# A fused transformer block on one core: loads of the opening split over two queues, and products of zeros while the weights load

## The chip, the core and the metric

The kernel runs on one core of a Trainium2 chip. The metric is the device time of one execution in microseconds, and lower is better. Before the change it is 466.33 us (median of 3 runs, 465.85 to 466.46).

## What is computed

x is 16 x 64 x 512 (1,024 tokens of width 512), the context is 16 x 512 x 512, all float32. Three residual stages follow each other, each on a layer norm of x:

```python
x = x + cross_attention(layernorm(x), ctx, top_k=32)
x = x + wave_attention(layernorm(x))
x = x + ternary_ffn(layernorm(x))
```

Only the first one matters for the change:

```python
q = query @ Wq.T + bq
k = mem_state @ Wk.T + bk
v = mem_state @ Wv.T + bv
scores = einsum('btd,bsd->bts', q, k) * scale
vals, idx = top_k(scores, 32)
scores = masked.at[b_ix, t_ix, idx].set(vals)
attn = softmax(scores)
return einsum('bts,bsd->btd', attn, v) @ Wo.T + bo
```

The wave attention convolves deposits over time with a kernel made of three small parameter vectors (frequency, damping, phase) and mixes its 16 heads by a 16 x 16 coupling matrix.

## The kernel before

The kernel is written out engine by engine. Every engine has its own program, in a fixed order, and the programs meet at semaphores. A wait on an engine holds back all that stands behind it on that engine.

Queries and keys are never formed apart. TensorE first multiplies the two weight matrices into one, M1 = Wq.T Wk (512 x 512), in four steps over slices of 128 rows: `m1_step(o)` (line 1265) waits until query slice o and key slice o (256 KB each) have landed, and issues four float32 products of 128 x 512 into banks 0 to 3. M1 is then split into a high part (ScalarE, `m_hi`, line 521) and a low part (VectorE, `m_lo`, line 843), and `q_product(n)` (lines 1250 to 1252) multiplies it with the transposed, normalised tokens. `q_product(0)` waits for each of the four low parts in turn.

TensorE's order in the opening is: m1_step 0, 1, 2; `turn_first` 0 to 3 (line 1257: transposes of the normalised token tiles `xn`); m1_step 3; two tiny groups (lines 1287, 1288) for a bias; turn_first 4 and 5; q_product(0); turn_first 6 and 7; q_product(1) and so on.

Tokens come in eight tiles of 128, loaded two at a time (`resid<-x`, 512 KB). For each, VectorE makes the statistics (lines 826, 828, 830), GpSimd the factor (lines 391, 393), ScalarE the normalised tile `xn` (line 503), TensorE turns it, ScalarE takes the high part (`xt_hi`, line 509) and VectorE the low part (`xt_lo`, line 835).

VectorE's order in the opening is:

```python
dve.wait_ge(par_in, 64)
dve.tensor_reduce(nmax[0:H, :], cpl[0:H, :], AX.X, ALU.max, negate=True).then_inc(cmax_ok, 1)
absolute(d, wpar[:, 1, :]).then_inc(sp_u, 1)
for o in range(DC):
    sumk_part(o)
    first_stats((2 * o, 2 * o + 1))
first_xt((0, 1, 2, 3))
for e in range(DC):
    m1_lo_part(e)
```

`par_in` counts the four small tables of the wave attention: `wpar` (three vectors, 8 KB each as spread over the partitions) and `cpl` (1 KB). `sumk_part(o)` (lines 859, 860) adds up key slice o, scaled by the bias columns in `cols` (6 KB), and waits for query and key slice o. GpSimd waits for `par_in` too, and then makes `targ` (lines 384, 386).

ScalarE's order: an activation table load (before line 514), two small exponentials (514, 516), xn 0 to 5, xt_hi 0 to 3, xn 6 and 7, four m_hi, xt_hi 4 to 7, then the parts of qT (line 538) between absolute sums of the feed-forward weights (`wab`, line 551).

All transfers are requested by SyncE, in program order: `first_loads(o)` for o = 0 to 3 (lines 280 to 287), three chunks of w1 (line 293, 1 MB each), `woraw` and a bias (303, 304), then the context (line 311).

Of the kernel before, what the change touches and what calls it, by code (L numbers as in the profile page):

```python
# [13 lines left out]
P = 128  # L14
# [3 lines left out]
H = 16  # L18
# [5 lines left out]
DC = D // P  # L24
# [15 lines left out]
def perceiver_kernel(nc, x, ctx, wq, wk, wv, woT, bo, wgT, bg, freq, damp, phase, coup, woutT, bout, w1T, w2T, b2,  # L40
                     small, out):
    st = ExitStack()
    with st:
# [27 lines left out]
        def f(ap):  # L71

            return ap.bitcast(F32)
# [11 lines left out]
        mix_hi = sb("mix_hi", [P, P], F32R)  # L85
# [15 lines left out]
        cols = sb("cols", [P, 3, DC])  # L101
# [56 lines left out]
        bank = [st.enter_context(nc.psum_tensor(f"bank{n}", [P, 512], F32)) for n in range(8)]  # L158

        small_in, tab_in, bo_in, wo_in, wv_in = map(sem, ("small_in", "tab_in", "bo_in", "wo_in", "wv_in"))
        wst_in = [sem(f"wst_in{n}") for n in range(4)]
        wab_in = [sem(f"wab_in{n}") for n in range(3)]
        wqk_in = [sem(f"wqk_in{n}") for n in range(DC)]
# [5 lines left out]
        consts, par_in, tpos_ok = sem("consts"), sem("par_in"), sem("tpos_ok")  # L170
# [39 lines left out]
        def rows(w):  # L210
            return w.rearrange("(c p) n -> p c n", p=P)
# [63 lines left out]
        @block.sync  # L275
        def _(sp):

            def first_loads(o):

                sp.dma_start(wqraw[:, o, :], rows(wq)[:, o, :]).then_inc(wqk_in[o], 16)  # L280
                sp.dma_start(wkraw[:, o, :], rows(wk)[:, o, :]).then_inc(wqk_in[o], 16)
                if o == 0:
                    sp.dma_start(cols[:, :, :], small[0]).then_inc(small_in, 16)
                    for n, a in enumerate((freq, damp, phase)):
                        sp.dma_start(wpar[:, n, :], a.partition_broadcast(P)).then_inc(par_in, 16)
                    sp.dma_start(cpl[0:H, :], coup).then_inc(par_in, 16)
                sp.dma_start(resid[:, 2 * o:2 * o + 2, :], x_v[:, 2 * o:2 * o + 2, :]).then_inc(x_in[o], 16)

            def abs_load(k):

                if k >= 3:
                    sp.wait_ge(abs_ok, k - 2)
                sp.dma_start(w_place(k, wab[:, k % 3, :]), w_chunk(k)).then_inc(wab_in[k % 3], 16)

            def ternary_load(k):

                sp.dma_start(w_place(k, wst[:, k % 4, :]), w_chunk(k)).then_inc(wst_in[k % 4], 16)

            for o in range(DC):
                first_loads(o)  # L300
            for k in range(3):
                abs_load(k)
            sp.dma_start(woraw[:, :, :], rows(woT)).then_inc(wo_in, 16)
            sp.dma_start(bias_x[:, :], bo.partition_broadcast(P)).then_inc(bo_in, 16)

            for b in range(B):
                for c in range(SC):
                    if b >= 4:
                        sp.wait_ge(ctx_turned, DC * (b - 3))
                        sp.wait_ge(nat_lo_ok, SC * (b - 4) + c + 1)  # L310
                    sp.dma_start(ctxr[:, b % 4, c, :], rows(ctx[b])[:, c, :]).then_inc(ctx_in[b % 4], 16)
                if b == 1:
                    for k in range(3, 2 * DC):
                        abs_load(k)
                    sp.dma_start(wvraw[:, :, :], rows(wv)).then_inc(wv_in, 16)
                if b == 3:
                    sp.dma_start(b1c[:, :], small[1]).then_inc(tab_in, 16)
                    sp.dma_start(bqg[:, :, :], small[2]).then_inc(tab_in, 16)

            for s, n in enumerate((2, 3, 0, 1)):  # L320
                sp.wait_ge(ctx_turned, DC * (B - 3 + s))
                sp.wait_ge(nat_lo_ok, SC * (B - 3 + s))
                sp.dma_start(wgraw[:, s, :, :], rows(wgT[n])).then_inc(wg_in[n], 16)
            sp.wait_ge(mt_used, 2 * DC * NT)
            sp.dma_start(bkb[:, :], bg[0].partition_broadcast(P)).then_inc(kvb_in, 16)
            sp.dma_start(bvb[:, :], bg[1].partition_broadcast(P)).then_inc(kvb_in, 16)
            for k in range(2 * DC):
                if k < 4:
                    sp.wait_ge(wg_lo_ok[w_slot(k)], DC)
                else:  # L330
                    sp.wait_ge(tern_ok, k - 3)
                ternary_load(k)
            sp.wait_ge(v_ps, NT)
            sp.dma_start(woutraw[:, :, :], rows(woutT)).then_inc(wout_in, 16)
            sp.dma_start(bias_o[:, :], bout.partition_broadcast(P)).then_inc(bout_in, 16)
            sp.wait_ge(conv_ps, H)
            sp.dma_start(bias_2[:, :], b2.partition_broadcast(P)).then_inc(b2_in, 16)
            for t in range(NT):
                sp.wait_ge(final_ok, t + 1)
                sp.dma_start(out_v[:, t, :], resid[:, t, :]).then_inc(stored, 16)  # L340
            sp.wait_ge(stored, 16 * NT)
# [3 lines left out]
        def _(pool):  # L345
            steps = [0]

            def link(ins):

                steps[0] += 1  # L350
                ins.then_inc(pool_step, 1)
                pool.wait_ge(pool_step, steps[0])

            link(pool.memset(ident[:, :], 0.0))
            pool.affine_select(out=ident[:, :], in_=ident[:, :], compare_op=ALU.not_equal, fill=1.0, base=0,
                               pattern=[[-1, P]], channel_multiplier=1).then_inc(consts, 1)
            pool.memset(neg_half[:, :], -0.5).then_inc(consts, 1)
            pool.memset(half_pi[:, :], TWO_PI / 4).then_inc(consts, 1)
            pool.memset(ones[:, :], 1.0).then_inc(consts, 1)  # L360
            pool.wait_ge(consts, 4)
            pool.tensor_tensor(fold[:, :], ident[:, 0:T], ident[:, T:P], ALU.add).then_inc(consts, 1)

            pool.wait_ge(consts, 5)
            for q in range(2):
                if q:
                    pool.wait_ge(tpos_ok, q)
# [128 lines left out]

        @block.scalar
        def _(act):
            def ln_apply(n, t, to):  # L500

                act.wait_ge(ln_rstd, 2 * n + 2)
                act.activation(to, resid[:, t, :], ACT.Identity, bias=ln_nb[:, n:n + 1],  # L503
                               scale=ln_rs[:, n:n + 1]).then_inc(ln_ready, 1)
# [60 lines left out]
            q_part(4)  # L565
            q_part(5)
            act.wait_ge(arg_ok, 1)
            act.wait_ge(consts, 5)
            act.activation(targ[:, :, :], targ[:, :, :], ACT.Sin, bias=half_pi[:, :], scale=-1.0).then_inc(cos_ok, 1)
            abs_part(4)  # L570
            q_part(6)
# [236 lines left out]
        def _(dve):  # L808
# [30 lines left out]
            d, u, z, z2, q, a = (wtmp[:, n, :] for n in range(6))  # L839
# [65 lines left out]
            for part in (PI_HI, PI_MID, PI_LO):  # L905
# [6 lines left out]
            link(dve.tensor_scalar(cpl[0:H, :], cpl[0:H, :], rinv[0:H, 0:1], None, ALU.mult))  # L912
            dve.tensor_copy(cpr[0:H, :].rearrange("p (h e) -> p h e", e=E8),
                            cpl[0:H, :].unsqueeze(2).to_broadcast([H, H, E8])).then_inc(cpr_ok, 1)
            dve.wait_ge(consts, 5)
            dve.tensor_reduce(mask8[:, :], ident[:, :].rearrange("p (h e) -> p e h", e=E8), AX.X,
                              ALU.add).then_inc(cpr_ok, 1)

# [328 lines left out]
        def _(pe):  # L1247
# [22 lines left out]
            def turn_first(t):  # L1270
# [3 lines left out]
                    pe.wait_ge(xt_lo_ok, t - 1)  # L1274
                turn(turn_bank(t), first_xn(t)).then_inc(xn_turned, 1)

            for o in range(DC - 1):
                m1_step(o)
            pe.wait_ge(consts, 5)
            for t in range(4):  # L1280
                turn_first(t)
            m1_step(DC - 1)
# [3 lines left out]
            for e in range(DC):  # L1286
                pe.matmul(bank[4][:, e:e + 1], sum_k[:, token(e)], ones[:, :], start=True, stop=True)
            pe.matmul(bank[4][:, DC:DC + 1], bqk1[:, :].to_broadcast([P, P]), ones[:, :], start=True,
                      stop=True).then_inc(qbias_ps, 1)
            def q_product(n):  # L1290
# [6 lines left out]
                for e in range(DC):  # L1297
                    if n == 0:
# [15 lines left out]
                      stop=True).then_inc(u_ps, 1)  # L1314
# [439 lines left out]
```

## Time and profile before

| | before |
|---|---|
| median of 3 runs | 466.33 us (465.85 to 466.46) |
| the profiled execution | 466.23 us |
| its span, first to last instruction | 464.5 us |
| TensorE busy | 447.9 us, 96% |
| VectorE, ScalarE, GpSimd busy | 70%, 55%, 49% |
| chain that ended last | TensorE 67%, VectorE 19%, ScalarE 5% |

The span is shorter than the execution's own time by what lies around the first and the last instruction, 1.7 us. The shares are averages over stages with different limits; how the first 24 us go is read from the timeline.

### The profile page before, as it was taken

Reading aid. Unit: us, or ns where it says so; the run is one execution under the profiler, and the core shown is the slowest. Engines: PE = TensorE matmul, PEld = TensorE weight load, DVE = VectorE, ACT = ScalarE, POOL = GpSimd, SP = SyncE. Lnnn points to the kernel's source line nnn. Section 1 sums busy time; section 2 is a strip of 40 time slices with the busy share of each in tenths; the row PEclk is TensorE's granted clock in tenths of the full one; section 3 lists DMA queues with packets and bytes.
Section 4 is the critical chain, followed back from the end, with each engine's and each line's share of the span. In section 5 each row is a group of like instructions: output and inputs, shape, how many; then the busy total and the mean of one; then the engine's idle time right before and its main releaser. Section 6 shows DMA issues by size and latency. Waiting matters only on the chain.

```text
span 464.5 us, 6292 instructions
## 1 busy us (share of the span) xinstructions
PE 447.9 (96%) x2146; PEld 352.8 (76%) x2146; DVE 326.9 (70%) x594; ACT 253.3 (55%) x392; POOL 226.2 (49%) x265
## 2 busy tenths in 40 slices
PE   6999989899999999889999999999999999999996
PEld 2588655588888888678888888888788888888884
DVE  4899679699999999978998893655872223522224
ACT  1777949577878887765787446443541221111111
POOL 6703098497779777834001761334226643333330
PEclk9999999999999999999999999999999999999999
DMA  7997733253444342570880300000000000100002
GB/s 222 414 370 286 260 105 113 69 159 122 127 138 131 118 117 90 182 226 1 338 289 11 110 1 23 1 0 0 2 0 0 1 0 1 68 23 1 0 1 91
DMA packets 23327, 48.94 MB, mean 105 GB/s; under 512 B 2688, under 2 KB 2688, under 8 KB 22272
## 3 DMA queue, kind: packets, MB, share of 16 engines
q1 hardware_dynamic: 23296, 48.55, 30.8%
q8 instruction: 17, 0.28, 0.2%
q14 instruction: 14, 0.11, 0.1%
HBM read 46.44 MB, written 2.10 MB: 105 GB/s over the span
## 4 chain that ended last, share of the span: by engine, by line
PE 67%; DVE 19%; ACT 5%; issue 4%; POOL 2%; DMA 2%; DVEq 0%; SPq 0%; ACTq 0%
PE bank L1250 10%; PE bank L1252 10%; PE bank L1251 10%; PE bank L1697 6%; PE bank L1699 6%; PE bank L1683 6%; PE bank L1684 6%; DVE mt_lo L1005 4%; PE bank L1265 4%; DVE work L1018 3%; DVE mx L1014 3%; PE bank L1257 2%; POOL nat_lo L428 2%; PE bank L1343 2%; DVE s_t L1025 1%
## 5 line engine op out<-in xcount | busy, mean ns | idle before, releaser
L428 POOL TENSOR_TENSOR nat_lo<-ctxr,nat_hi 128x512 fp32r<-128x512 f32 x64 | 83.9, 1338 | 21.0 <-ACT nat_hi L612 20.6
L801 ACT ACTIVATE g<-bank,b1c 128x512 f32<-128x512 f32 x32 | 22.1, 689 | 92.2 <-PE bank L1699 92.2
L1230 DVE CAST g_hi<-g 128x512 fp32r<-128x512 f32 x32 | 13.9, 434 | 74.9 <-ACT g L801 74.8
L483 POOL TENSOR_SCALAR w2s<-w2t 128x512 fp32r<-128x512 int8 x32 | 19.9, 621 | 65.9 <-PE bank L1684 65.9
L1697 PE MATMUL bank<-xt_lo,w1s 128*128 128x512 f32 x128 | 50.8, 397 | 0.0
L1699 PE MATMUL bank<-xt_hi,w1s 128*128 128x512 f32 x128 | 50.7, 396 | 0.0
L1683 PE MATMUL bank<-w2s,g_lo 128*128 128x512 f32 x128 | 50.2, 392 | 0.2 <-DVE g_lo L1232 0.2
L1684 PE MATMUL bank<-w2s,g_hi 128*128 128x512 f32 x128 | 50.2, 392 | 0.0
L588 ACT ACTIVATE mt_hi<-bank 128x512 fp32r<-128x512 f32 x64 | 37.8, 595 | 18.6 <-PE bank L1423 18.2
L1005 DVE TENSOR_TENSOR mt_lo<-bank,mt_hi 128x512 fp32r<-128x512 f32 x64 | 43.5, 681 | 4.7 <-ACT mt_hi L588 4.4
L1423 PEld LDWEIGHTS bank<-ident,ctxr 128*128 128x128 f32 x256 | 30.5, 141 | 12.9 <-issue 4.9
L612 ACT ACTIVATE nat_hi<-ctxr 128x512 fp32r<-128x512 f32 x64 | 36.6, 624 | 5.6 <-PE bank L1455 5.6
L1423 PE MATMUL bank<-ident,ctxr 128*128 128x128 f32 x256 | 38.6, 275 | 0.6 <-DMA ctxr<-ctx 0.4
L1437 PE MATMUL bank<-mt_lo,qs 128*128 128x512 f32 x64 | 30.3, 473 | 0.0
L391 POOL TENSOR_TENSOR ln_rs<-ln_ve,neg_half 128x1 f32<-128x1 f32 x24 | 14.6, 606 | 32.2 <-DVE ln_ve L830 31.7
L503 ACT ACTIVATE xn<-resid,ln_nb,ln_rs 128x512 f32<-128x512 f32 x24 | 19.3, 814 | 19.1 <-POOL ln_nb L393 18.6
L1683 PEld LDWEIGHTS bank<-w2s,g_lo 128*128 128x128 f32 x128 | 24.0, 188 | 6.0 <-issue 0.6
L1699 PEld LDWEIGHTS bank<-xt_hi,w1s 128*128 128x128 f32 x128 | 24.0, 188 | 5.6
L1684 PEld LDWEIGHTS bank<-w2s,g_hi 128*128 128x128 f32 x128 | 24.0, 188 | 5.6
L1697 PEld LDWEIGHTS bank<-xt_lo,w1s 128*128 128x128 f32 x128 | 24.0, 188 | 5.5
L1453 PE MATMUL bank<-nat_lo,at 128*128 128x512 f32 x64 | 25.3, 395 | 1.4 <-issue 0.9
L472 POOL TENSOR_TENSOR qfT<-qfT,gate 128x512 f32<-128x512 f32 x8 | 10.4, 1296 | 32.7 <-ACT gate L769 32.7
(234 smaller groups left out, 1205.8 us busy)
## 6 DMA issues: line engine op xcount, KB each, us to landing
ctxr<-ctx SPq DMA_DIRECT2D x64, 256.0 KB, 2.8
wab<-w1T SPq DMA_DIRECT2D x4, 1024.0 KB, 10.4
wab<-w2T SPq DMA_DIRECT2D x4, 1024.0 KB, 5.7
wgraw<-wgT SPq DMA_DIRECT2D x4, 1024.0 KB, 5.3
wst<-w1T SPq DMA_DIRECT2D x4, 1024.0 KB, 7.6
wst<-w2T SPq DMA_DIRECT2D x4, 1024.0 KB, 7.1
resid<-x SPq DMA_DIRECT2D x4, 512.0 KB, 6.3
out<-resid SPq DMA_DIRECT2D x8, 256.0 KB, 2.2
```

The source lines that it names most:

```text
L428: pool.tensor_tensor(nat_lo[:, par, c, :], ctxr[:, b % 4, c, :], f(nat_hi[:, par, c, :]), ALU.subtract).then_inc(nat_lo_ok, 1)
L588: act.activation(mt_hi[:, g % 4, :], ctx_bank(g)[:, :], ACT.Copy).then_inc(mt_hi_ok, 1)
L612: act.activation(nat_hi[:, par, c, :], ctxr[:, b % 4, c, :], ACT.Copy).then_inc(nat_hi_ok, 1)
L1005: dve.tensor_tensor(mt_lo[:, g % 4, :], ctx_bank(g)[:, :], f(mt_hi[:, g % 4, :]), ALU.subtract).then_inc(mt_lo_ok, 1)
L1250: pe.matmul(to, w_hi, x_lo, start=first, stop=False)
L1251: pe.matmul(to, w_lo, x_hi, start=False, stop=False)
L1252: return pe.matmul(to, w_hi, x_hi, start=False, stop=last)
L1423: ins = pe.transpose(ctx_bank(g)[:, token(c)], ctxr[:, b % 4, c, token(d)], ident[:, :])
L1683: pe.matmul(to, g_lo[:, n % 2, token(k)], w2s[:, n % 2, :], start=(c == 0), stop=False)
L1684: ins = pe.matmul(to, g_hi[:, n % 2, token(k)], w2s[:, n % 2, :], start=False, stop=(c == FC - 1))
L1697: pe.matmul(bank[n % 2][:, :], w1s[:, n % 2, d, :], xt_lo[:, d, half(n // FC)], start=(d == 0), stop=False)
L1699: ins = pe.matmul(bank[n % 2][:, :], w1s[:, n % 2, d, :], xt_hi[:, d, half(n // FC)], start=False, stop=(d == DC - 1))
```

## The change

ScalarE requests the four key slices and the five small tables, ahead of everything else in its program: key slice 0, the tables, key slices 1 to 3. SyncE requests the query slices and x in the order q0, x0, q1, q2, x1, q3, x2, x3. GpSimd first sets the tile `mix_hi` (128 x 128) to zero, and TensorE multiplies that tile by itself five times, in float32, into bank 7, before it waits for the first slices. The semaphore `consts` therefore counts one step more. `mix_hi` gets its real content much later (line 948), and bank 7 is written afresh by turn_first(3).

```diff
-            def first_loads(o):
+            def query_load(o):
 
                 sp.dma_start(wqraw[:, o, :], rows(wq)[:, o, :]).then_inc(wqk_in[o], 16)
-                sp.dma_start(wkraw[:, o, :], rows(wk)[:, o, :]).then_inc(wqk_in[o], 16)
-                if o == 0:
-                    sp.dma_start(cols[:, :, :], small[0]).then_inc(small_in, 16)
-                    for n, a in enumerate((freq, damp, phase)):
-                        sp.dma_start(wpar[:, n, :], a.partition_broadcast(P)).then_inc(par_in, 16)
-                    sp.dma_start(cpl[0:H, :], coup).then_inc(par_in, 16)
+
+            def x_load(o):
+
                 sp.dma_start(resid[:, 2 * o:2 * o + 2, :], x_v[:, 2 * o:2 * o + 2, :]).then_inc(x_in[o], 16)
...
-            for o in range(DC):
-                first_loads(o)
+            query_load(0)
+            x_load(0)
+            query_load(1)
+            query_load(2)
+            x_load(1)
+            query_load(3)
+            x_load(2)
+            x_load(3)
...
+            pool.memset(f(mix_hi[:, :]), 0.0).then_inc(consts, 1)
             link(pool.memset(ident[:, :], 0.0))
...
         @block.scalar
         def _(act):
+            def key_load(o):
+
+                act.dma_start(wkraw[:, o, :], rows(wk)[:, o, :]).then_inc(wqk_in[o], 16)
+
+            key_load(0)
+            act.dma_start(cols[:, :, :], small[0]).then_inc(small_in, 16)
+            for n, a in enumerate((freq, damp, phase)):
+                act.dma_start(wpar[:, n, :], a.partition_broadcast(P)).then_inc(par_in, 16)
+            act.dma_start(cpl[0:H, :], coup).then_inc(par_in, 16)
+            for o in range(1, DC):
+                key_load(o)
+
...
+            pe.wait_ge(consts, 1)
+            for n in range(5):
+                pe.matmul(bank[7][:, 0:P], f(mix_hi[:, :]), f(mix_hi[:, :]), start=True, stop=True)
             for o in range(DC - 1):
                 m1_step(o)
-            pe.wait_ge(consts, 5)
+            pe.wait_ge(consts, 6)
```

SyncE's requests at the start of its program, before (`wqraw`, `wkraw` are query and key slices, `resid` the tokens, `wab` the w1 chunks):

```order
L280 DMA wqraw<-wq 128x512
L281 DMA wkraw<-wk 128x512
L283 DMA cols<-attn_bias_cols 128x12
L285 DMA wpar<-freq 128x16
L285 DMA wpar<-damp 128x16
L285 DMA wpar<-phase 128x16
L286 DMA cpl<-coup 16x16
L287 DMA resid<-x 128x2x512
L280 DMA wqraw<-wq 128x512
L281 DMA wkraw<-wk 128x512
L287 DMA resid<-x 128x2x512
```

and of the changed kernel:

```order
L280 DMA wqraw<-wq 128x512
L284 DMA resid<-x 128x2x512
L280 DMA wqraw<-wq 128x512 x2
L284 DMA resid<-x 128x2x512
L280 DMA wqraw<-wq 128x512
L284 DMA resid<-x 128x2x512 x2
L290 DMA wab<-w1T 128x2048 x3
```

The nine requests of keys and tables are gone from this queue, and the first x stands second instead of eighth.

ScalarE at the start of its program in the changed kernel (before, it began with the table load):

```order
L506 DMA wkraw<-wk 128x512
L509 DMA cols<-attn_bias_cols 128x12
L511 DMA wpar<-freq 128x16
L511 DMA wpar<-damp 128x16
L511 DMA wpar<-phase 128x16
L512 DMA cpl<-coup 16x16
L506 DMA wkraw<-wk 128x512 x3
L530 ACT_TABLE_LOAD
L530 ACTIVATE wtmp<-wtmp 128x16 [waits sp_u]
```

`cpl`, the last table, is the sixth request of its queue here and was the seventh of SyncE's, and the table load now stands behind nine requests.

## Rows read from the trace of the kernel before

**Rows 1.** The page, part 1: busy time and share of the span
```profile
PE 447.9 (96%) x2146; PEld 352.8 (76%) x2146; DVE 326.9 (70%) x594; ACT 253.3 (55%) x392; POOL 226.2 (49%) x265
```
**Rows 2.** Timeline from 0 to 24: SyncE's requests (start us, us, queue line, tile)
```profile
0.79 0.37 SPq L280 DMA_DIRECT2D wqraw<-wq  x1
1.22 0.42 SPq L281 DMA_DIRECT2D wkraw<-wk  x1
...
3.58 0.43 SPq L286 DMA_DIRECT2D cpl<-coup  x1
...
5.03 0.43 SPq L281 DMA_DIRECT2D wkraw<-wk  x1
...
8.35 0.64 SPq L281 DMA_DIRECT2D wkraw<-wk  x1
```
**Rows 3.** DMA issues at 1.2, 3.6 and 5.0 us: KB, us to landing
```profile
wqraw<-wq SPq DMA_DIRECT2D x1, 256.0 KB, 2.4
wkraw<-wk SPq DMA_DIRECT2D x1, 256.0 KB, 2.9
...
cpl<-coup SPq DMA_DIRECT2D x1, 1.0 KB, 2.6
...
wkraw<-wk SPq DMA_DIRECT2D x1, 256.0 KB, 4.6
```
**Rows 4.** Windows: busy PE, PEld, DVE, ACT, POOL; PEclk, DMA share, GB/s
```profile
4.00:5.00 1.00, 0.84 (x1) 0.50 (x2) 0.32 (x2) 0.00 (x0) 0.00 (x0) 1.00 0.13 14
...
10.00:11.00 1.00, 1.00 (x4) 0.38 (x3) 0.93 (x4) 0.00 (x0) 0.92 (x2) 1.00 1.06 387
```
**Rows 5.** Timeline: TensorE's weight loads in m1_step 0 and 1
```profile
5.17 0.34 PEld L1265 LDWEIGHTS bank<-wkraw,wqraw 128*128 128x128 f32 x1 [0.52 <-issue]
6.03 0.34 PEld L1265 LDWEIGHTS bank<-wkraw,wqraw 128*128 128x128 f32 x1 [0.52 <-issue]
...
8.59 0.34 PEld L1265 LDWEIGHTS bank<-wkraw,wqraw 128*128 128x128 f32 x1 [0.52 <-issue]
9.28 0.19 PEld L1265 LDWEIGHTS bank<-wkraw,wqraw 128*128 128x128 f32 x1 [0.36 <-issue]
9.71 0.19 PEld L1265 LDWEIGHTS bank<-wkraw,wqraw 128*128 128x128 f32 x1 [0.24 <-DMA wkraw<-wk]
```
**Rows 6.** Timeline: VectorE from the tables on, GpSimd beside it
```profile
6.32 0.16 DVE L873 TENSOR_REDUCE nmax<-cpl 16x1 f32<-16x16 f32 x1 [1.67 <-DMA cpl<-coup]
6.36 2.18 POOL L384 TENSOR_TENSOR targ<-wpar,tpos 128x1152 f32<-128x1152 f32 x1 [3.11 <-DMA cpl<-coup]
...
6.49 2.34 DVE L859 TENSOR_SCALAR sum_k<-wkraw,cols 128x512 f32<-128x512 f32 x1
...
26.36 0.47 DVE L859 TENSOR_SCALAR sum_q<-wqraw,cols 128x512 f32<-128x512 f32 x1
```
**Rows 7.** Timeline: the way to m_hi (ScalarE) and m_lo (VectorE)
```profile
18.02 0.82 ACT L503 ACTIVATE xn<-resid,ln_nb,ln_rs 128x512 f32<-128x512 f32 x1 [0.62 <-POOL ln_nb L393]
...
22.06 2.07 ACT L521 ACTIVATE m_hi<-bank 128x512 fp32r<-128x512 f32 x4
...
22.70 2.48 DVE L843 TENSOR_TENSOR m_lo<-bank,m_hi 128x512 fp32r<-128x512 f32 x4 [0.86 <-ACT m_hi L521]
```
**Rows 8.** The chain that ended last, from 22 to 44 us (start, us, what)
```profile
22.35 0.79 PE bank L1287 x8
...
24.29 0.24 PE bank L1250
...
43.55 1.28 ACT L569
```
**Rows 9.** Timeline: GpSimd's first memset, ScalarE's table load and first activation
```profile
0.79 0.20 POOL L355 MEMSET ident<- 128x128 f32 x1 [0.29 <-POOLq L1744]
0.80 1.28 ACT L514 ACT_TABLE_LOAD   x1 [0.80 <-PEq L1744]
...
6.59 0.21 ACT L514 ACTIVATE wtmp<-wtmp 128x16 f32<-128x16 f32 x1 [4.52 <-DVE wtmp L822]
```

More of the change, by code:

```diff
@@ L360, in _ @@
             pool.memset(ones[:, :], 1.0).then_inc(consts, 1)
-            pool.wait_ge(consts, 4)
+            pool.wait_ge(consts, 5)
             pool.tensor_tensor(fold[:, :], ident[:, 0:T], ident[:, T:P], ALU.add).then_inc(consts, 1)
-            pool.wait_ge(consts, 5)
+            pool.wait_ge(consts, 6)
             for q in range(2):
@@ L567, in _ @@
             act.wait_ge(arg_ok, 1)
-            act.wait_ge(consts, 5)
+            act.wait_ge(consts, 6)
             act.activation(targ[:, :, :], targ[:, :, :], ACT.Sin, bias=half_pi[:, :], scale=-1.0).then_inc(cos_ok, 1)
@@ L914, in _ @@
                             cpl[0:H, :].unsqueeze(2).to_broadcast([H, H, E8])).then_inc(cpr_ok, 1)
-            dve.wait_ge(consts, 5)
+            dve.wait_ge(consts, 6)
             dve.tensor_reduce(mask8[:, :], ident[:, :].rearrange("p (h e) -> p e h", e=E8), AX.X,
```

## The prediction

> **What bounds the kernel now.** I read the views from the whole to the place of the change: the page's busy shares, the timeline of the first 24 us by engine, the time from request to landing of single transfers, DMA traffic by microsecond, and the chain that ended last.
>
> TensorE is busy for 96% of the span [rows 1], so only time at the front that TensorE really gets back, or waits of others that end earlier, can shorten the run. In the opening four things matter.
>
> First, SyncE requests everything: query slice 0 at 0.79, key slice 0 at 1.22, then five small tables, the last (cpl) at 3.58, and the next key slice only at 5.03 [rows 2]. Key slice 0 lands 2.9 us after its request, 4.12; cpl 2.6 after, 6.18; key slice 1 4.6 after, 9.63 [rows 3]. By 8.35 a request costs 0.64 us instead of some 0.4 [rows 2]. Between 4 and 5 us the DMA engines move 14 GB/s, while from 10 to 11 they move 387 [rows 4]. That hole is the time in which SyncE asked for tables.
>
> Fourth, there is a second path, through VectorE. It waits for the last table, starts at 6.32, spends 2.34 us on the first row sum (line 859) while GpSimd runs line 384 from 6.36 to 8.54, and goes on, hardly pausing, through the row sums and the statistics of the eight tiles [rows 6]. The same row sum alone takes 0.47 [rows 6]. ScalarE follows with xn 5 at 18.02 and, behind the high parts of xT and two more xn, reaches m_hi at 22.06. VectorE makes the first m_lo from 22.70 on [rows 7]. Four take 2.48, so the first is done at about 23.3. TensorE's q_product(0) needs it and starts at 24.29 [rows 8]. With 0.3 us for the semaphore and a weight load (0.19), it could have started at 23.6 to 23.7. So VectorE's path has **0.65 us of slack** to TensorE's, no more.
>
> After that TensorE's products lead the chain until ScalarE takes over with its table load at 43.55 [rows 8], and the chain goes through ScalarE and VectorE into the attention. Whatever q_product(0) gains is therefore handed on; I find no fixed clock or transfer behind it that would stop it.
>
> **The change part by part.** My sum is made against the profiled execution, 466.23 us with a span of 464.5; the median of the runs is 466.33, so I add 0.10 at the end. A difference of 0.2%, 0.93 us, is about what a measurement here can tell.
>
> *Key slice 0 by ScalarE.* No row shows a transfer requested by ScalarE. It is free at 0.80 (its table load starts there [rows 9]), and a request costs SyncE 0.37 to 0.64 [rows 2]. Query and key slices are then asked for at about 0.8 each. The query slice took 2.4, the key slice behind it 2.9 [rows 3], so both lie between 3.2 and 3.7. I take 3.6: 0.56 before 4.16. The ends are a gain of 0.96, and nothing if the two hinder each other.
>
> *Zeros.* GpSimd's memset of mix_hi stands first; its neighbour on ident, of the same size, takes 0.20 from 0.79 [rows 9], so TensorE starts at about 1.1. Five products are ten records. The lower bound is line 1287's record, 0.79/8 = 0.10 us at the full clock, twice that at the low one: 2.0 us in all. The upper bound is a quarter of 0.86 (128 columns for 512) plus a bare weight load of 0.34: 0.55 each, 5.5 us. In rows 5 the loads run beside the products, so I take 2.1 and an end at 3.2, before the slices. At 5.5 the real work would start at 6.6 with the clock up, and end within 0.1 us of today. If 4.95 us of work raise the clock here too, it rises at 6.05. From 3.6 that leaves 2.45 slow us, which hold 2.85 records; 21.15 at 0.43 end at 15.1, where today's 24 records end at 17.0. **TensorE's path gains about 1.9.** If the zeros do not count, it gains the 0.56 of the start alone. The multiplied values are never read: bank 7 is overwritten.
>
> *Data for that pace.* TensorE would want slice 1 at about 8.4, slice 2 at 11.8, and slice 3 after the four turns at 17. ScalarE asks for key slice 1 seventh, at 0.8 + 6 x 0.47 = 3.6. If the two queues share the 387 GB/s evenly, key 1 (256 KB at half of that, 1.35 us) lands near 7. If everything is served in order of request, 2.5 MB come before its end, 6.8 us at 387 from 2.4 on: 9.2. That would cut TensorE's gain to 1.1. Query 3 and x are requested 4 to 5 us earlier than today.
>
> *Tables by ScalarE.* cpl is the sixth request of its queue, not the seventh: 0.48 earlier. That is the upper end for VectorE's path. For the lower end, a request costing 0.64 each time would put cpl at 4.3 (0.7 later), and traffic on the other queue, which these tables did not meet before (they ran through the hole), could add what key 1 shows over key 0, 1.7. Nearest is cpl's own row, 2.6, with the same key slice ahead of it; I add 0.23 for the new neighbour. **VectorE's path gains 0.25**, with ends of +0.48 and -2.4.
>
> *What waits behind ScalarE's nine requests.* Its table load (1.28) ends at 0.8 + 9 x 0.47 + 1.28 = 6.3, and its first activation started at 6.59 [rows 9], behind VectorE. The normalisations need it only past 11. Nothing is lost there. GpSimd's 0.2 us is hidden too: it waits for the tables until 6.36. SyncE reaches the w1 loads 5 us earlier, and nobody needs those before 29.
>
> *Sum.* TensorE could be at q_product(0) at 24.29 - 1.9 = 22.4, but m_lo allows it only 0.65 + 0.25 = **0.9 us** earlier than now. Hence 466.23 - 0.9 = 465.33, plus 0.10: 465.4. Of the 1.9 us that the opening seems to offer, a full microsecond stops at VectorE's path.
>
> **The rivals.**
>
> *A. Shared DMA engines delay the tables: slower.* Both queues end on the same 16 engines. For it speaks that the tables now compete with 2.5 MB of x and queries; against it, that a table of 1 KB and a slice of 256 KB take about the same time to land, 2.6 and 2.4 to 2.9, so that a request alone is latency and hardly engine time [rows 3]. Suppose that the engines alternate whole requests. At 387 GB/s 256 KB last 0.68 and x 1.35. Between 3.8 and the fifth table stand x 0, queries 1 and 2, x 1 and query 3: 4.7 us, so cpl lands near 8.5, 2.3 later than now. Minus the slack of 0.65 this makes the kernel 1.65 slower: 468.0. A milder sharing with cpl at 7.2 costs 0.4. The point of decision is cpl's landing at 6.8. The Trainium skill, DMA: Bandwidth & Descriptors, section Queues, rings and completion order, says that an engine serves the queues in turn and drains a whole packet from one before it switches; by that rule the result would be this rival's. Chance 0.16.
>
> *B. About nothing, 466.1.* The tables land up to 0.5 later than now, or key slice 1 comes at 9.5 (TensorE's gain 0.9, less with a zeros block that ends late). A gain of 0 to 0.5. Chance 0.24.
>
> *C. VectorE's path gets shorter, 464.7.* If VectorE's first row sum comes in ahead of GpSimd's line 384, it takes 0.47 and not 2.34, and the slack becomes 2.5; TensorE's path then decides, with 1.9 at most and 1.6 with a little late data. Against it: both wait for the same tables, and VectorE has two small instructions ahead of that sum, as now. Chance 0.14.
>
> *Forecast.* A gain of 0.6 to 1.13 us, 465.2 to 465.7. Chance 0.46.
>
> **How the numbers follow.** The forecast's interval is cut by the 0.93 us in its upper part, so 0.30 of its 0.46 I count as faster; with C that makes 0.44. The rest of it and B make 0.40, and A 0.16. The range goes from C's 464.7 to the milder form of A, 466.8; outside are A's hard form and a gain above 1.6.
>
> **What would show it.** Right: ten zero records from about 1.1 to 3.2; m1_step at 3.6; 0.43 per record from about 6; VectorE's line 873 a few tenths before 6.32; **TensorE idle ahead of the first q_product, released by m_lo**, which is the mark of this prediction. Wrong: no such wait (C, or TensorE's path was slower than worked out), line 873 later than 6.8 (A), a wait for key slice 1 past 9.4, or slow records as long as before, which would mean that zeros do not raise the clock.

## The result and the profile after

The changed kernel takes **470.42 us** (median of 4 runs, 470.1 to 471.23), against 466.38 for the kernel before, measured again beside it (465.85 to 466.46). The ratio is 1.0087, with a 95% interval of 1.0069 to 1.0106: **4.0 us slower**, where 0.9 faster was forecast. The profiled execution took 470.54 us with a span of 468.7. The page of the changed kernel, part 1 (busy time and share of the span), answers to [rows 1]:

```profile
PE 451.3 (96%) x2156; PEld 354.8 (76%) x2156; DVE 325.0 (69%) x594; ACT 253.4 (54%) x392; POOL 226.4 (48%) x266
```

The shares tell nothing: TensorE's 3.4 us of additional busy time are for the most part the ten records of zeros (2.5). The loss has to be found in the opening.

DMA issues of the changed kernel, three narrow stretches from 0.8, 3.3 and 3.9 us on (KB, us from request to landing), beside [rows 3]:

```profile
wkraw<-wk ACTq DMA_DIRECT2D x1, 256.0 KB, 3.1
wqraw<-wq SPq DMA_DIRECT2D x1, 256.0 KB, 3.5
...
wqraw<-wq SPq DMA_DIRECT2D x1, 256.0 KB, 8.7
cpl<-coup ACTq DMA_DIRECT2D x1, 1.0 KB, 7.2
...
resid<-x SPq DMA_DIRECT2D x1, 512.0 KB, 10.8
wkraw<-wk ACTq DMA_DIRECT2D x1, 256.0 KB, 7.9
```

SPq marks SyncE's requests, ACTq ScalarE's. cpl holds 1 KB. It took 2.6 us before and takes 7.2 now. Key slice 1 took 4.6 and takes 7.9. The first pair lands at 3.9 (key) and 4.3 (query), so it is complete 0.2 us later than before (4.12). What the two queues ask for lands side by side: bias columns and x 0 at 5.6 and 5.8, frequency and query 1 at 7.7 and 7.5, damping and query 2 at 8.9 and 8.4, phase by itself at 9.8, cpl and x 1 at 10.5 and 10.7, key 1 and query 3 at 11.8 and 12.0.

The timeline of the changed kernel by engine (start us, us, engine, line): ScalarE's requests, TensorE's weight loads, and VectorE and GpSimd from the tables on. It answers to [rows 2, 5, 6]:

```profile
0.79 0.41 ACTq L506 DMA_DIRECT2D wkraw<-wk  x1
...
1.05 2.21 PEld L1295 LDWEIGHTS bank<-mix_hi 128*128 128x128 f32 x10 [1.05 <-POOL mix_hi L358]
...
3.32 0.52 ACTq L512 DMA_DIRECT2D cpl<-coup  x1
...
3.87 1.67 ACTq L506 DMA_DIRECT2D wkraw<-wk  x3
...
4.36 0.50 PEld L1281 LDWEIGHTS bank<-wkraw,wqraw 128*128 128x128 f32 x2 [1.10 <-DMA wqraw<-wq]
...
8.79 0.28 PEld L1281 LDWEIGHTS bank<-wkraw,wqraw 128*128 128x128 f32 x1 [0.52 <-issue]
9.32 0.19 PEld L1281 LDWEIGHTS bank<-wkraw,wqraw 128*128 128x128 f32 x1 [0.24 <-issue]
10.59 0.16 DVE L889 TENSOR_REDUCE nmax<-cpl 16x1 f32<-16x16 f32 x1 [4.59 <-DMA cpl<-coup]
10.63 2.11 POOL L388 TENSOR_TENSOR targ<-wpar,tpos 128x1152 f32<-128x1152 f32 x1 [7.23 <-DMA cpl<-coup]
10.67 2.10 DVE L838 SCALAR_TENSOR_TENSOR wtmp<-wpar 128x16 f32<-128x16 f32 x1
...
11.86 0.30 PEld L1281 LDWEIGHTS bank<-wkraw,wqraw 128*128 128x128 f32 x2 [2.35 <-DMA wkraw<-wk]
...
12.69 0.47 DVE L875 TENSOR_SCALAR sum_k<-wkraw,cols 128x512 f32<-128x512 f32 x1
```

VectorE's chain starts at 10.59, released by cpl, and not at 6.32: 4.27 us late. TensorE is late on its own account too: key slice 1 releases it at 11.86, not 9.71. And the zeros, which run from 1.05 to 3.26, did nothing for the clock: the loads still last 0.34 until 8.8 and the clock rises at about 9.0, within 0.1 us of where it rose before. (That the two are so close is a coincidence of two executions, as the experiments show.) The collision with GpSimd is there as before, only that it now hits the small instruction of line 838 (2.10) and spares the row sum (0.47), the other way round than in [rows 6]; the sum of the two is about the same (2.57 against 2.49).

The chain that ended last in the changed kernel, the pieces that matter (start, length, what), answers to [rows 8]:

```profile
3.32 7.16 DMA cpl<-coup
...
27.04 0.70 DVE m_lo L859
27.88 0.47 PE bank L1266
...
47.37 1.28 ACT L585
```

The chain runs through VectorE's path, as forecast for the gain: cpl, statistics, xn, m_hi, m_lo. TensorE waits 0.9 us for m_lo and starts q_product(0) at 27.88. By the timeline it started at 24.05 before, which is 3.83 earlier (24.29, in [rows 8], is where the chain view lets that piece begin). The line of the kernel before and that of the changed one:

```profile
24.05 0.48 PE L1250 MATMUL bank<-xt_lo,m_hi 128*128 128x512 f32 x1
```

```profile
27.88 0.47 PE L1266 MATMUL bank<-xt_lo,m_hi 128*128 128x512 f32 x1 [0.93 <-DVE m_lo L859]
```

The table load of ScalarE follows 3.82 later than before. VectorE's first top-8 is 3.78 late (69.67 and 73.45), so the delay is handed on undiminished. It is 3.6 at 176 us and 4.2 from 186 us to the end. What adds 0.6 there need not be this change: measured by the same top-8 steps against the same profile of the kernel before, the kernel with the zeros alone goes from 1.16 to 1.75 late in that stretch, while the one with eight ones, below, shows no step (0.51 early on both sides). Its cause is open.

Windows of the changed kernel (busy PE, PEld, DVE, ACT, POOL; granted clock, DMA share, GB/s) answer to [rows 4]:

```profile
6.00:7.00 1.00, 1.00 (x2) 0.34 (x1) 0.00 (x0) 0.85 (x1) 0.00 (x0) 1.00 0.39 110
...
8.00:9.00 1.00, 1.00 (x3) 0.48 (x2) 0.00 (x0) 0.00 (x0) 0.00 (x0) 1.00 0.67 194
```

I had expected full traffic here, because nothing stands in SyncE's way any more. Instead the rate dips from 6 to 7 us and again from 8 to 9, while the tables are on their way; between the dips it is 325 GB/s.

### The profile page after: what moved, and what is told of

It reads as the page before. It is cut to its first block, busy times and chain, and to the rows that moved or that the text cites. A ratio compares the mean times of both kernels' runs of the same rounds, so it can differ in the third digit from the quotient of the medians.

```text
span 468.7 us, 6313 instructions
## 1 busy us (share of the span) xinstructions
PE 451.3 (96%) x2156; PEld 354.8 (76%) x2156; DVE 325.0 (69%) x594; ACT 253.4 (54%) x392; POOL 226.4 (48%) x266
## 4 chain that ended last, share of the span: by engine, by line
PE 65%; DVE 18%; ACT 6%; issue 5%; DMA 3%; POOL 2%; ACTq 1%; DVEq 0%; SPq 0%
PE bank L1266 10%; PE bank L1268 10%; PE bank L1267 10%; PE bank L1716 6%; PE bank L1718 6%; PE bank L1702 6%; PE bank L1703 6%; DVE mt_lo L1021 3%; DVE work L1034 3%; DVE mx L1030 2%; PE bank L1273 2%; POOL nat_lo L432 2%; PE bank L1442 2%; DMA ctxr<-ctx 2%; DVE ln_s L842 2%
## 5 line engine op out<-in xcount | busy, mean ns | idle before, releaser
L519 ACT ACTIVATE xn<-resid,ln_nb,ln_rs 128x512 f32<-128x512 f32 x24 | 19.3, 814 | 17.2 <-POOL ln_nb L397 16.7
```

## The experiments

Each kernel below was measured beside runs of the kernel before on the same chip, whose median was 466.6 to 466.8. Ratios are to these.

### What delays the tables, and does ScalarE's queue matter?

**Zeros alone**, the kernel before with the memset and the five products:

```diff
+            pool.memset(f(mix_hi[:, :]), 0.0).then_inc(consts, 1)
...
+            pe.wait_ge(consts, 1)
+            for n in range(5):
+                pe.matmul(bank[7][:, 0:P], f(mix_hi[:, :]), f(mix_hi[:, :]), start=True, stop=True)
```

> The kernel before plus the zeros alone (loads as before). Theory (loads): the zeros raise TensorE's clock near 6 us, m1_step 0 ends earlier, but key slice 1 still lands at 9.63, so TensorE waits there and everything after stands where it stood: 466.4 us, at most 0.3 less. Rival (the zeros themselves cost the time of the change): about 470.4.

Measured: 467.12 us, ratio 1.0018 (1.0003 to 1.0033). No gain, and a loss of 0.8 us by the ratio, 0.1 to 1.5 by its interval: far from the 4 us, though not shown to be nothing. And the reason was not the one expected: in its profile the clock rose only at about 10.5, so m1_step 0 never got faster. The profile also says how much one landing is worth: its requests are those of the kernel before at the same times, and cpl took 3.2 us instead of 2.6.

**Loads alone**, the changed kernel without the five products:

```diff
-            pe.wait_ge(consts, 1)
-            for n in range(5):
-                pe.matmul(bank[7][:, 0:P], f(mix_hi[:, :]), f(mix_hi[:, :]), start=True, stop=True)
```

> The changed kernel without the five products of zeros. Theory: VectorE's path behind cpl (landing at 10.5) sets the end, TensorE's clock does not matter, so 470.4 us, within 0.3. Rival (zeros cost or give something in the changed kernel): off by over 0.5.

Measured: 471.39 us, ratio 1.0099 (1.0080 to 1.0119), an interval that overlaps that of the changed kernel. The whole loss is there without the zeros, so it lies in the loads. But the median is 0.97 above 470.4, and "off by over 0.5" was the mark of the rival. The trace shows where the excess comes from in the profiled execution. VectorE starts at 10.81 and q_product(0) at 28.0, only 0.2 us later than in the changed kernel; then TensorE runs it slowly. Windows of this kernel (granted clock, DMA share and GB/s last):

```profile
28.00:29.00 1.00, 0.97 (x2) 0.83 (x3) 1.00 (x3) 1.00 (x4) 0.00 (x0) 0.50 1.06 389
```

Towards the end of the wait of 0.9 us for m_lo the clock fell to half, and it stayed there until 31: seven steps from one weight load to the next take 0.43 us instead of 0.23. The first top-8 is 5.4 us late, against 3.8 in the changed kernel, where a wait of the same length left the clock at 1.00. The same wait had two outcomes in two profiles; whether the missing zeros have a part in that is not shown.

**Tables requested by SyncE**, keys left to ScalarE:

```diff
             query_load(0)
+            sp.dma_start(cols[:, :, :], small[0]).then_inc(small_in, 16)
+            for n, a in enumerate((freq, damp, phase)):
+                sp.dma_start(wpar[:, n, :], a.partition_broadcast(P)).then_inc(par_in, 16)
+            sp.dma_start(cpl[0:H, :], coup).then_inc(par_in, 16)
             x_load(0)
...
             key_load(0)
-            act.dma_start(cols[:, :, :], small[0]).then_inc(small_in, 16)
...
```

> The changed kernel, but the five tables are requested by SyncE behind query slice 0 and ahead of x; the key slices stay with ScalarE. Theory (the tables are slow because another queue is full beside them): ScalarE's four key slices, 1 MB, are now that neighbour; cpl lands at 7 to 8 and the time is 467 to 468. Rival (ScalarE's queue serves small tables badly): cpl lands at 5.7, 465.5 us.

Measured: 469.94 us, ratio 1.0077 (1.0054 to 1.0100). DMA issues of this kernel at 3.1 us:

```profile
wpar<-phase SPq DMA_DIRECT2D x1, 8.0 KB, 5.8
cpl<-coup SPq DMA_DIRECT2D x1, 1.0 KB, 7.1
```

The same queue that landed cpl in 2.6 us before needs 7.1 now, with key slices on the other queue. So ScalarE's queue is not to blame: it is the neighbour. But cpl came at 10.2, not at 7 to 8, and the time was not 467 to 468; I had priced the neighbour too low a second time.

**x waits for the tables**, queues as in the changed kernel:

```diff
             query_load(0)
+            sp.wait_ge(small_in, 16)
+            sp.wait_ge(par_in, 64)
             x_load(0)
```

> The changed kernel, but SyncE waits until the tables have landed before it requests x 0 and what follows. Theory (neighbour): the tables, with only query slice 0 and key slice 0 beside them, land at 5.8; x 0 lands near 9.7 and query slice 1 near 10.6, which cost VectorE's and TensorE's paths about 1 us, so 467.2 us. Rival (ScalarE's queue serves small tables badly whatever is beside it): cpl still lands past 9, and with the later loads 472 or more.

Measured: 468.45 us, ratio 1.0041 (1.0028 to 1.0055). DMA issues of this kernel at 3.1 us, and VectorE's first instruction behind the tables in its timeline:

```profile
wpar<-phase ACTq DMA_DIRECT2D x1, 8.0 KB, 3.0
cpl<-coup ACTq DMA_DIRECT2D x1, 1.0 KB, 3.5
```

```profile
6.79 0.16 DVE L891 TENSOR_REDUCE nmax<-cpl 16x1 f32<-16x16 f32 x1 [1.91 <-DMA cpl<-coup]
```

This is the decisive run: the same five requests on the same queue of ScalarE, and cpl lands in 3.5 us instead of 7.2, because SyncE's queue is silent. The time is 1.3 above the 467.2 expected. What is left of the loss, 1.9 us, I read as the late data that was accepted with the edit: x 0 landed at 10.8 instead of 9.7, and TensorE waits for query slice 1 until 11.43 in this profile.

**Thinner tables**, 32 partitions instead of 128. This kernel is for timing only; it leaves out the parameters on the other 96 partitions:

```diff
-                act.dma_start(wpar[:, n, :], a.partition_broadcast(P)).then_inc(par_in, 16)
+                act.dma_start(wpar[0:32, n, :], a.partition_broadcast(32)).then_inc(par_in, 16)
```

> The changed kernel, but each of the three parameter vectors is loaded to 32 partitions instead of 128 (the other rows of wpar hold 1.0, so that the wave kernel's tables are left out on them; the number and order of instructions behind stay): 2 small packets per DMA engine and table instead of 8. Theory A1 (every small packet costs a turn of its own): cpl lands near 7.5 and key slice 1 near 9, 467.0 us. Theory A2 (the engines alternate whole requests, whatever their size): cpl still at 10.5, 470.4 us.

Measured: 469.36 us, ratio 1.0059 (1.0039 to 1.0078). DMA issues at 3.3 us:

```profile
wqraw<-wq SPq DMA_DIRECT2D x1, 256.0 KB, 7.6
cpl<-coup ACTq DMA_DIRECT2D x1, 1.0 KB, 6.9
```

Between the two theories, but nearer to A2. The vectors themselves came 1.2 to 1.6 us earlier (frequency at 6.5 instead of 7.7, phase at 8.2 instead of 9.8), so a table's many small packets have a price; cpl, behind them, came at 10.2 and not at 7.5. Most of the delay is waiting behind data of the other queue.

**Nothing waits for the tables**: the same loads as in the changed kernel, but the wait for `par_in` moved.

```diff
+            for o in range(DC):
+                sumk_part(o)
+                first_stats((2 * o, 2 * o + 1))
             dve.wait_ge(par_in, 64)
             dve.tensor_reduce(nmax[0:H, :], cpl[0:H, :], AX.X, ALU.max, negate=True).then_inc(cmax_ok, 1)
             absolute(d, wpar[:, 1, :]).then_inc(sp_u, 1)
-            for o in range(DC):
-                sumk_part(o)
-                first_stats((2 * o, 2 * o + 1))
...
```

(GpSimd's `targ` moves behind its eight factors, ScalarE's two exponentials behind xt_hi 5.)

> The changed kernel with its loads and zeros as they are, but VectorE, GpSimd and ScalarE do their work on the tables behind the eight tiles' statistics, so that nothing in the opening waits for cpl. Theory: then only TensorE's wait for key slice 1 (11.8 against 9.7) is left, 468.5 us against 470.4. Rival (the late cpl alone makes the loss, TensorE's wait is covered): 466.4. Rival (cpl is not what holds VectorE's path up): 470.4.

Measured: 468.48 us, ratio 1.0032 (1.0018 to 1.0047). Its timeline at key slice 1:

```profile
11.66 0.75 DVE L876 SCALAR_TENSOR_TENSOR sum_k<-wkraw,cols,sum_k 128x512 f32<-128x512 f32 x1 [2.74 <-DMA wkraw<-wk]
11.68 0.30 PEld L1281 LDWEIGHTS bank<-wkraw,wqraw 128*128 128x128 f32 x2 [1.72 <-DMA wkraw<-wk]
```

468.5 was expected. In this profile nothing waits for m_lo: the first one starts at 23.50, and TensorE reaches q_product(0) on its own at 25.70. The loss of the change thus has two layers. By the ratios, 1.0087 and 1.0032 (from different sets of runs, so with some tenths of doubt), some 2.5 us are VectorE's wait for cpl, and below it lie 1.5 us because key slice 1 comes at 11.7 instead of 9.6.

### The data in time, and the zeros

**Late tables on one queue**, with five zeros. VectorE, GpSimd and ScalarE as in the last kernel, and all requests on SyncE's queue. In the kernel as run x 2 stands ahead of the four tables, not behind them as the expectation lists it:

```diff
                 sp.dma_start(wkraw[:, o, :], rows(wk)[:, o, :]).then_inc(wqk_in[o], 16)
                 if o == 0:
                     sp.dma_start(cols[:, :, :], small[0]).then_inc(small_in, 16)
+                if o < 3:
+                    sp.dma_start(resid[:, 2 * o:2 * o + 2, :], x_v[:, 2 * o:2 * o + 2, :]).then_inc(x_in[o], 16)
+                if o == 2:
                     for n, a in enumerate((freq, damp, phase)):
                         sp.dma_start(wpar[:, n, :], a.partition_broadcast(P)).then_inc(par_in, 16)
                     sp.dma_start(cpl[0:H, :], coup).then_inc(par_in, 16)
...
```

> A version meant to beat both: all loads on SyncE's queue (query 0, key 0, cols, x 0, query 1, key 1, x 1, query 2, key 2, the four tables of par_in, x 2, query 3, key 3, x 3), the zeros kept, and VectorE, GpSimd and ScalarE do their work on the tables behind the eight tiles' statistics instead of ahead of them. If the tables and the missing data were what held the opening up, x 0 lands near 5.6 and key 1 near 7, TensorE is at q_product(0) 1.5 to 1.9 us earlier than before: 464.5 to 464.9 us. Rival (time saved in the opening is lost behind it, or the zeros do not raise the clock in time): 466 or more.

Measured: 466.77 us, ratio 1.0000 (0.9989 to 1.0011). The gain expected did not come. x 0 landed at 6.8 and key 1 at 8.3, VectorE had m_lo ready in time, and TensorE's loads still ran at the low clock until about 9.3. Its timeline:

```profile
1.05 2.21 PEld L1284 LDWEIGHTS bank<-mix_hi 128*128 128x128 f32 x10 [1.05 <-POOL mix_hi L359]
4.13 0.50 PEld L1270 LDWEIGHTS bank<-wkraw,wqraw 128*128 128x128 f32 x2 [0.87 <-DMA wkraw<-wk]
...
8.56 0.33 PEld L1270 LDWEIGHTS bank<-wkraw,wqraw 128*128 128x128 f32 x1 [0.52 <-issue]
9.37 0.19 PEld L1270 LDWEIGHTS bank<-wkraw,wqraw 128*128 128x128 f32 x1 [0.47 <-issue]
```

**The same without zeros** (the five products and the memset left away):

> The same without the zeros. Theory: TensorE then runs its first 4.9 us at the low clock as before, and its path to q_product(0) is as long as before: 466.4 us. Rival (the zeros are worth nothing even when the data is there): equal to the version with zeros.

Measured: 466.99 us, ratio 1.0003 (0.9990 to 1.0016). The same as with five zeros. The rival holds: five zeros are worth nothing that the runs can tell, even when the data is there. By the lengths of the records, the clock rose between 7.5 and 10.6 in the profiles with five zeros and between 7.4 and 9.1 in the three without. That scatter is part of what sets two executions of one kernel apart: here it rose at 7.7, and q_product(0)'s first weight load came at 23.37, against 24.02 with a rise at 9.1 in the kernel before.

**Late tables on two queues** (the changed kernel's loads, but ScalarE asks for the four tables of par_in last; the three engines work on the tables late, as above):

```diff
             key_load(0)
             act.dma_start(cols[:, :, :], small[0]).then_inc(small_in, 16)
+            for o in range(1, DC):
+                key_load(o)
             for n, a in enumerate((freq, damp, phase)):
                 act.dma_start(wpar[:, n, :], a.partition_broadcast(P)).then_inc(par_in, 16)
             act.dma_start(cpl[0:H, :], coup).then_inc(par_in, 16)
-            for o in range(1, DC):
-                key_load(o)
```

> The changed kernel with its two queues and zeros, but ScalarE requests key 0, cols, keys 1 to 3 and only then the four tables, and the three engines do the work on the tables behind the statistics. Theory (small packets slow the traffic of both queues while they run): the slices that TensorE needs are ahead of them, so 464.5 to 465.2. Rival (two queues are slower than one by themselves): 466 or more, above the version with one queue by over 1 us.

Measured: 467.18 us, ratio 1.0011 (0.9998 to 1.0023), neither the gain expected nor clearly above the version with one queue. Two queues as such do no harm that is clear of noise; here too the clock was low until about 8.6.

**Eight zeros** and **eight ones**, on the version with late tables on one queue:

```diff
-            for n in range(5):
+            for n in range(8):
```

and for the second also

```diff
-            pool.memset(f(mix_hi[:, :]), 0.0).then_inc(consts, 1)
+            pool.memset(f(mix_hi[:, :]), 1.0).then_inc(consts, 1)
```

> The version with late tables on one queue (466.8 us with five products of zeros), with eight of them: at 0.44 us each they last from 1.05 to 4.6, so that TensorE has no pause before the first slices. Theory P (five products did not raise the clock because they ended 0.9 us before the real work): the clock now rises before 8 us in the profile and the time is 465.3 to 465.8. Theory Z (zeros do not count as work, however many): the clock rises where it rose without them, 8 to 10 us, and the time is 466.8 to 467.2, the real work starting 0.3 later.

> The same with the tile set to 1.0 instead of 0.0. Theory P: as with eight zeros. Theory Z: here the clock rises before 8 us and the time is 465.3 to 465.8, over 0.8 less than with eight zeros.

Measured: 465.49 us, ratio 0.9976 (0.9957 to 0.9996) with zeros; 465.34 us, ratio 0.9968 (0.9954 to 0.9981) with ones. The timeline of the kernel with eight zeros:

```profile
1.05 3.37 PEld L1284 LDWEIGHTS bank<-mix_hi 128*128 128x128 f32 x16 [1.05 <-POOL mix_hi L359]
4.33 0.30 PEld L1270 LDWEIGHTS bank<-wkraw,wqraw 128*128 128x128 f32 x2
4.88 0.19 PEld L1270 LDWEIGHTS bank<-wkraw,wqraw 128*128 128x128 f32 x1 [0.24 <-issue]
5.31 0.19 PEld L1270 LDWEIGHTS bank<-wkraw,wqraw 128*128 128x128 f32 x1 [0.24 <-issue]
...
8.25 0.30 PEld L1270 LDWEIGHTS bank<-wkraw,wqraw 128*128 128x128 f32 x2 [1.04 <-DMA wkraw<-wk]
```

Theory P's numbers came, and Theory Z is out. With three products more there is no pause ahead of the first real load (no idle time stands behind the second line, where the kernel with five has 0.87); the clock is up at 4.3 with zeros and by 5.2 with ones, and a record of m1_step 0 takes 0.43. Zeros do it as well as ones. That it was the pause which spoilt the five is argued, not shown: the eight differ from them in number and in the pause at once, and no run has eight products that end early. The last line shows what comes next: TensorE now outruns the data and waits 1.04 us for key slice 1. **Both versions beat the kernel before**, by 1.1 us (0.2 to 2.0) with zeros and 1.5 us (0.9 to 2.1) with ones. Eight products in the changed kernel itself, with its early tables, were not run.

**Thin tables in the late version**, with five zeros, again for timing only:

```diff
-                        sp.dma_start(wpar[:, n, :], a.partition_broadcast(P)).then_inc(par_in, 16)
+                        sp.dma_start(wpar[0:32, n, :], a.partition_broadcast(32)).then_inc(par_in, 16)
```

> The version with late tables on one queue and five zeros, each parameter vector to 32 partitions only (the other rows of wpar hold 1.0, which leaves out the wave kernel's tables there). In that version the DMA engines moved 81 and 15 GB/s from 11 to 13 us, between x 1 and x 2. Theory H (the tables' many small packets make the hole, 16 engines at some 250 packets a microsecond whatever their size): 144 of 384 such packets fewer per... in numbers 384 become 96, the hole shrinks from 2 us to about 1 and x 3 lands 1 us earlier; the time stays, since TensorE's path sets it. Rival (the hole is the time of the requests on the queue): the hole stays 2 us.

Measured: 467.31 us, ratio 1.0001 (0.9988 to 1.0015). Windows of the late version with full tables, and then with thin ones (last two columns: DMA share, GB/s):

```profile
11.00:12.00 1.00, 1.00 (x4) 0.43 (x3) 0.93 (x4) 0.42 (x2) 0.80 (x3) 1.00 0.26 81
12.00:13.00 1.00, 1.00 (x4) 0.52 (x3) 0.97 (x2) 0.69 (x1) 0.92 (x1) 1.00 0.14 15
```

```profile
11.00:12.00 1.00, 1.00 (x4) 0.42 (x3) 0.93 (x4) 0.47 (x2) 0.80 (x3) 1.00 1.08 353
12.00:13.00 1.00, 1.00 (x4) 0.39 (x3) 0.97 (x2) 0.72 (x1) 0.95 (x1) 1.00 1.04 375
```

Theory H, and more clearly than its own number: the hole is gone altogether, and x 3 lands at 15.0 instead of 16.7. In this version it was not the time of the requests, which had all been made by 9.2. The time of the kernel stays, as expected, since TensorE's path sets it.

## Why the prediction was wrong

The case that came is rival A, to which I had given 0.16, and it came harder than I had priced it: cpl at 10.5, not 8.5.

- **Tables by ScalarE: the step that failed.** "Nearest is cpl's own row, 2.6, with the same key slice ahead of it; I add 0.23 for the new neighbour." It took 7.2: 4.6 us more, not 0.23. The run in which x waits shows that the neighbour makes the difference, and the run with the tables on SyncE's queue that the issuing engine does not. The 0.25 us of gain was besides smaller than the scatter of one landing (2.6 and 3.2 us for the same requests). The stated lower end of -2.4 was too mild as well. It came from key slice 1, which met only requests ahead of it on its own queue. Rival A had worked out 8.5, and the same number comes out if everything is served in order of request: ahead of cpl stand five slices and two x, 2.36 MB, which last 6.1 us at 387 GB/s from 2.4 on. What adds the last two microseconds is open. The dips in the rate look like the tables' own cost, but with thin tables, which have less of it, cpl still came at 10.2. And the order of request does not hold: query 3 was requested just before cpl and landed 1.5 us after it, and with the tables on SyncE's queue only five slices stood ahead of cpl, which gives 5.8, and it came at 10.2. The landings in pairs look more like two queues served in turns, one request of each, which is how rival A reckoned; no run separates the two.
- **The hole between 4 and 5 us.** I read it as "the time in which SyncE asked for tables". That is not all of it. In the late version the requests behind the tables had long been made, and the rate fell all the same for two microseconds, and did not with thin tables: serving the tables costs traffic. In the kernel before, the two cannot be told apart, since x 0 was requested only at 4.05, and the first traffic of all, behind the request at 0.79, came between 1.75 and 2.0. What the prediction left out is that the change would carry the tables' own cost into the traffic.
- **Key slice 1.** Two estimates stood there, 7 (queues share evenly) and 9.2 (order of request), and the sum went by a gain that needs about 9.4 at the latest. It landed at 11.8, beside query 3 and behind the tables. With the tables out of VectorE's way this alone makes 1.5 us, and the point at which it decides was in the text.
- **VectorE's path, slack 0.65.** The mechanism was right and its size nearly: the first m_lo starts 4.34 later (22.70 and 27.04), and q_product(0) moved by 3.83, so the slack was 0.51. The 0.65 came out near by two errors that cancel in part: the start was read from the chain view as 24.29 instead of 24.05, and 0.3 us was allowed from m_lo to TensorE where 0.14 was needed. The wait of TensorE for m_lo, "the mark of this prediction", is there with 0.9 us. It marks the limit, not the sign: it stands behind a late m_lo as behind an early one.
- **Zeros.** The duration was right, 1.05 to 3.26, predicted 1.1 to 3.2. That they end before the slices I had counted as harmless; "if 4.95 us of work raise the clock here too" passed over the pause, 1.10 us. The time went as in the fall-back, "if the zeros do not count", but that is not the reason: eight of them do count. TensorE's path gained nothing at all rather than 1.9: its start at 4.36 is later than 4.16, against the 0.56 earlier that I had counted.
- **Handing on** held: 3.83 at 28 us, 3.78 at 70 us, 4.2 at the end. With eight zeros the profile is 1.36 early at 70 us and 0.7 at the end; the difference arises in the same late stretch, whose cause is open.
- **Covers** held: ScalarE's nine requests, GpSimd's memset and SyncE's early w1 loads cost nothing that shows; no run takes one of them away by itself.

The Trainium skill, DMA: Bandwidth & Descriptors, section Issuing engines are not separate DMA queues, says that requests from several engines run on the same 16 DMA engines and interleave, and that a second issuing engine only saves time on the sequencer. The traces agree: the last x was requested 4.7 us earlier and landed 0.8 earlier (15.8 against 16.6), and cpl, requested 0.26 us earlier, landed 4.3 later.

## What to carry to other kernels

Before a load is moved to another queue, list everything that is requested ahead of it on all queues, in bytes, and divide by the full rate. Take the result as a floor: here it came 1.7 to 4.4 us short (8.5 for 10.5 and 10.2, 5.8 for 10.2), but even as a floor it would have stopped this change. A small table on which an engine's whole program waits pays for the megabytes beside it. If a table is needed early, let it run while nothing else does; if it is not, put its consumer behind the work that does not need it. Let products for the clock reach up to the real work: here eight did and gave 1.1 to 1.5 us, together with late tables, and five that ended 0.8 to 1.3 us before it gave nothing.

## What the runs showed of the hardware

- Tables spread over many partitions cost traffic out of all proportion to their bytes. In the late version the rate is 81 and then 15 GB/s for two microseconds while the four tables, 25 KB, are served; with three of them on a quarter of the partitions it is 353 and 375 GB/s. The engines' busy share is 0.26 and 0.14 in those two microseconds, so this cost does not show as busy time.
- Two queues with tables on one and slices on the other move less than the full rate: with the tables on SyncE's queue and the keys on ScalarE's it was 100 to 200 GB/s from 4 to 8 us, at a busy share of 0.4 to 0.8. With large pieces on both queues (the late version with two queues) it was 320 to 401 from 5 to 10 us. Why cpl, 1 KB, lands up to 2 us behind phase in these mixed stretches is open; in the quiet ones it is 1 us or less.
- Products of zeros count as work for TensorE's clock: with eight of them it is at 2.4 GHz instead of 1.2 when the real work begins, and with eight of ones soon after. Behind five of them and a pause of 0.8 to 1.3 us it stayed low for 3.1 to 6.2 us of real work. That the rise comes at a different distance each time fits what the Trainium skill, TensorE: Matmul & The Clock Gate, Part 1, says: what watches the engine's activity runs freely and does not start with the kernel. In the opening the granted clock of the windows read 1.00 all the while, and only the length of the records tells the two levels apart. Later it does tell: in the profile of the loads alone it read 0.50 from 28 to 31 us, beside records of the slow length.
- A wait of 0.9 us left TensorE's clock at 0.50 in that profile and at 1.00 in the changed kernel's. The low stretch of 3.3 us made seven steps 0.2 us longer each, 1.4 us in all.
